# Attention with experts: two gates on SyncE's DMAs, at the query and the key group

## What is computed

```python
x = L0_attn_x                                   # [32, 512, 256], fp32
xn = layernorm(x)
# attention, 16 heads of 16, no softmax:
q, k, v = xn @ Wq + bq, xn @ Wk + bk, xn @ Wv + bv      # split into heads
scores = einsum('bhid,bhjd->bhij', q, k) * decay_mask   # 0.95 ** (i - j), causal
out = einsum('bhij,bhjd->bhid', scores, v)
attn = groupnorm(out @ Wo + bo) * gamma + beta          # a group is a head, over all positions
# 8 experts, each takes the 128 best of the 512 rows of each batch:
probs = softmax(xn @ gate_w)
top_p, top_idx = top_k(probs.T, 128)
ffn = scatter_add(top_idx, top_p * (gelu(xn[top_idx] @ w1) @ w2))
return x + attn + ffn
```

## Time and profile before

| what | us |
|---|---|
| median of three executions | 2489.22 (2487.41 to 2489.69) |
| the profiled execution | 2482.65 |
| its span, first to last instruction | 2480.8 |
| PE busy | 2323.8 (94%) |
| PEld, DVE, POOL, ACT busy | 2024.0, 1305.8, 1277.9, 990.0 |
| DMA share of the queue of SyncE's transfers (q1) | 10.8% of 16 engines |

### The profile page before, as it was taken

The page is one execution under the profiler, slowest core; times in us unless marked ns, Lnnn a source line. Parts: engine busy times, 40 slices in busy tenths (PEclk is TensorE's granted clock), DMA queues, the critical chain, the costliest instruction groups (busy, mean ns, idle before and its releaser), DMA issues.

```text
span 2480.8 us, 76765 instructions
## 1 busy us (share of the span) xinstructions
PE 2323.8 (94%) x31948; PEld 2024.0 (82%) x31948; DVE 1305.8 (53%) x2531; ACT 990.0 (40%) x1801; POOL 1277.9 (52%) x2088
## 2 busy tenths in 40 slices
PE   6999999889999995899999999999999999999997
PEld 5777777777777773789999999999999999999996
DVE  2455545466655556764455445545544554555443
ACT  4555555555545552333333333333333333333332
POOL 4334344433343342556666666666666666665453
PEclk9999999999999997899999999999999999999998
DMA  3122222222222211322332323323223323223222
GB/s 121 54 85 73 71 71 74 85 71 78 72 79 71 71 54 50 91 43 47 78 51 44 80 47 63 65 44 82 42 49 78 49 44 81 47 47 47 45 49 26
DMA packets 129262, 156.22 MB, mean 63 GB/s; under 512 B 11008, under 2 KB 118656, under 8 KB 129024
## 3 DMA queue, kind: packets, MB, share of 16 engines
q0 software_dynamic: 49152, 67.14, 16.7%
q1 hardware_dynamic: 79872, 85.54, 10.8%
HBM read 85.53 MB, written 67.11 MB: 62 GB/s over the span
## 4 chain that ended last, share of the span: by engine, by line
PE 58%; POOL 1%; DVE 1%; issue 0%; DMA 0%; ACT 0%; POOLq 0%; DVEq 0%; ACTq 0%
PE hidden L1295 28%; PE y L1310 27%; PE xt L1282 2%; POOL out L1148 0%; POOL xg L1138 0%; DMA out<-y,scatter_idx 0%; DVE best_index L204 0%; DVE g_hi L1262 0%; DVE best L200 0%; DMA xg<-xn_rows,step_idx 0%; DVE g_lo L1264 0%; DVE rows L208 0%; DVE xt_lo L1251 0%; ACT y L1197 0%; ACT g L1211 0%
## 5 line engine op out<-in xcount | busy, mean ns | idle before, releaser
L1148 POOL DMA_INDIRECT out<-y,scatter_idx x256 | 430.7, 1683 | 412.1 <-ACT y L1197 352.6
L1262 DVE CAST g_hi<-g 128x512 fp32r<-128x512 f32 x512 | 289.7, 566 | 667.6 <-ACT g L1211 665.2
L1310 PE MATMUL y<-w_hi,g_hi 128*128 128x256 f32 x2048 | 571.3, 279 | 0.3 <-ACT y L1197 0.3
L1310 PE MATMUL y<-w_lo,g_hi 128*128 128x256 f32 x2048 | 565.8, 276 | 0.0
L1310 PE MATMUL y<-w_hi,g_lo 128*128 128x256 f32 x2048 | 565.6, 276 | 0.0
L1211 ACT ACTIVATE g<-hidden 128x512 f32<-128x512 f32 x512 | 306.8, 599 | 402.9 <-PE hidden L1295 402.9
L1295 PE MATMUL hidden<-xt_hi,w_lo 128*128 128x512 f32 x1024 | 404.5, 395 | 0.0
L1295 PE MATMUL hidden<-xt_lo,w_hi 128*128 128x512 f32 x1024 | 402.7, 393 | 0.0
L1295 PE MATMUL hidden<-xt_hi,w_hi 128*128 128x512 f32 x1024 | 399.5, 390 | 1.5 <-DVE xt_lo L1251 1.5
L1264 DVE TENSOR_TENSOR g_lo<-g,g_hi 128x512 fp32r<-128x512 f32 x512 | 386.2, 754 | 17.6
L1310 PEld LDWEIGHTS y<-w_hi,g_hi 128*128 128x128 f32 x2048 | 384.6, 188 | 0.5 <-ACT y L1197 0.5
(11 more groups left out here) (150 smaller groups left out, 3615.1 us busy)
## 6 DMA issues: line engine op xcount, KB each, us to landing
x<-in_x SPq DMA_DIRECT2D x32, 512.0 KB, 5.6
w_stage<-in_w SPq DMA_DIRECT2D x16, 1024.0 KB, 6.1
xn_rows<-xn SPq DMA_DIRECT2D x32, 512.0 KB, 3.7
res<-in_x SPq DMA_DIRECT2D x32, 512.0 KB, 4.0
out<-res SPq DMA_DIRECT2D x32, 512.0 KB, 2.9
xg<-xn_rows,step_idx POOLq DMA_INDIRECT x256
out<-y,scatter_idx POOLq DMA_INDIRECT x256, 3.9
cst<-in_cst SPq DMA_DIRECT2D x1, 436.0 KB, 4.2
```

The source lines that it names most:

```text
L1148: pool.indirect_dma_start(out_rows, bass.IndirectOffsetOnAxis(sidx[:, k:k + 1], 0), y[:, k, :], None, compute_op=ALU.add).then_inc(scatter ...
L1262: dve.tensor_copy(g_hi[:, m, :], g32[m % 4][:]).then_inc(gh_ready, 1)
L1310: last = pe.matmul(yb[k % 2][:, 0:D], g_[:, m, cols], w[par][:, m, :], start=i == 0, stop=i == 3 * FT - 1)
```

## The change

The pair xn store and x load moves from the pass of its norm to the start of the next pass, and gets a wait for the first query group of that pass. The output store and the residual load behind it get a wait for the third group, the first key group. No instruction of another engine changes.

```diff
             def one(b, par):
+                f, l = b + 1, b + 1
+
+                if has(f):
+                    sp.wait_ge(qk_mm, 4 * f + 1)
+                if has(l):
+                    sp.wait_ge(xn_ready, TT * l + TT)
+                    sp.dma_start(xn_v[l], xn[:]).then_inc(xn_stored, 16)
+                    if has(l + 2):
+                        sp.dma_start(xb[1 - par][:], x_v[l + 2]).then_inc(x_in[1 - par], 16)
+                if has(f):
+                    sp.wait_ge(qk_mm, 4 * f + 3)
                 if has(b - 2):
                     sp.wait_ge(res_ready, 2 * b - 2)
...
                     sp.wait_ge(out_stored, max(16 * b - 16, 0))
                     sp.dma_start(res[:], x_v[b - 1]).then_inc(res_in, 16)
-                if has(b + 2):
-
-                    sp.wait_ge(xn_ready, TT * b + 3 * TT)
-                    sp.dma_start(xn_v[b + 2], xn[:]).then_inc(xn_stored, 16)
-                    if has(b + 4):
-                        sp.dma_start(xb[par][:], x_v[b + 4]).then_inc(x_in[par], 16)
```

## The result

The changed kernel took 2425.64 us, median of four executions (2415.68 to 2427.84), against 2488.31 (2482.38 to 2489.69): a ratio of 0.9747, 95% interval 0.9725 to 0.9768. That is 62.7 us less. The forecast was 2439 with a range of 2412 to 2470. The profiled execution is the fastest of the four, 2415.68 us (span 2413.9), so its trace shows some 67 us less than the one of before; where I compare traces, that is to be kept in mind.

What follows compares the result with a forecast made beforehand. The prediction took TensorE as the bound in attention, waiting for its own code, delayed by data traffic. From 2489.2 us it took 39 (stops) + 13 (clock) - 2 (new cost) = 50 us, giving 2439, range 2412 to 2470.

Steps and rivals of the forecast that it cites:

- Single stops: Attention passes with one TensorE stop for code, 2.45 us in the pass cited: expected to shrink to 1.55 us.
- the quiet pass: Attention pass after xn's stores and x's loads have run out: TensorE still stopped 1.87 us, with slow clock.
- The passes of the other kind: Attention passes with two TensorE stops, 1.14 and 1.52 us: expected to keep 1.1 us in all.
- second stops: Later stop in two-stop attention passes, 1.52 us: expected to fall to nothing, with 0.2 us allowed for a small third.
- first stops: Earlier stop in two-stop attention passes, 1.14 us: expected to keep 0.9 us, its code packet having started before the data.
- The clock: TensorE's lower clock in the 30 passes, costing 26 us: half, 13 us, expected back, bounds 0 and 26.
- the new cost: Residual load delaying code for the block ending near 403.8, every other pass: 2 us expected, bounds 0 and 15.
- near range: Whole kernel: 2426 to 2452 us around the forecast of 2439, given chance 0.55.
- (a): Attention stops: single ones fall only to 1.87 us and keep slow clock, second ones go; 2460 us, chance 0.22.
- (b): Attention code fetch: slow by itself, data beside it chance, so nothing moves; 2489 us, chance 0.07.
- (c): Attention: single stops stay and a late residual load adds stops at the block ending near 403.8; 2526 us, chance 0.06.
- (d): Attention passes: nearly all stops and all the clock loss go; 2412 us, chance 0.10.

Runs made afterwards that it cites:

- e5: Changed kernel plus two 512 KB DRAM-to-DRAM copies at the old place of xn store and x load, touching no tile: 2477.89 us.
- e7: Changed kernel with 162 waits on an already reached semaphore instead of one ahead of TensorE's first matmul, adding 80 instructions: 2448.16 us.
- e9: Kernel before, SyncE's old order, with only TensorE's fourth value group moved between the first two quarters of scores times values: 2460.87 us.
- e2: Kernel before with only the output store's wait for the key group added; xn store and x load stay: 2491.66 us.
- e1: Changed kernel without the output store's wait for the key group; xn store and x load still moved: 2425.57 us.

## Why the prediction was right

**The bound and the cause.** PE bound, waiting for its own code, delayed by data beside it: e5 shows that traffic alone brings the stops back, e7 that they follow the blocks. The "mostly hidden" of the Trainium skill (Runtime: NRT & Kernel Launch, Instruction fetch mechanics) stays untrue here, with 36.4 us left with no traffic beside them.

**The stops.** Expected 39 us saved, measured 42.1 (78.5 to 36.4), in the second trace of the changed kernel 38.1. Under this sum two errors partly cancel, which is luck. Single stops, expected 1.55, came out between 0.5 and 1.5, 1.10 in the mean of the table above, so 0.45 too high. About half of that is the work in the block: the prediction took 2.0 us, though its own block start near 403.9 and stop at 406.05 give over 2.1, and the table has 2.2. Its 1.1 from block start to packet is 0.9, its 2.45 from packet to resumption 2.4. I had leaned towards the quiet pass, whose 1.87 was a slow sample: no stop of the changed kernel's first trace is over 1.5. The passes of the other kind, expected at 1.1, kept 1.25 in the mean. Their second stops went as expected: L920's 14.3 us became 1.7. Their first stops stayed, at 0.9 on the average of a pass from 350 us on (0.5 to 1.1), and a third was left in some, up to 0.97.

**The clock.** This term was mis-sized: half of 26 us was expected, and 26.4 (61.4 x 0.43) came back in the profiled execution, 22 in the second (10.2 us left). The half was a hedge: the prediction had seen the clock fall behind a stop of 1.87 and put its own 1.55 below that. The runs bear out no such bound: the clock fell behind a stop of 1.68 in the second trace of the changed kernel and behind 1.25 in e9, and held behind 1.47 in the first. That all of it came back there is in part luck. The term accounts for 9 to 13 of the 13 us by which 2439 was too high. In the profiled execution, for which the forecast was 17 too high, 13.4 are the clock, 3.1 the stops and 2 the new cost, while 2.2 were lost in the column "remains" of the ledger.

**The range.** 2425.64 lies in the range of 2412 to 2470, and just at the low edge of the near range, 2426 to 2452, that had been given 0.55.

**New costs.** 2 us expected at the block that is wanted 0.3 us after its packet is in; no stop stands before L857's or L874's successors (L862, L879) in the 30 passes, so 0. Nobody came late for xn, x or res: no such wait is in PE's list, though the last data lands up to 14.9 us into a pass instead of before 14.5.

**The rivals.** (a), 2460, fell with the single stops. (b) and (c) needed the traffic to be chance; e5 rules that out, and the residual load never met the block that (c) names: in those passes the last data is in by +13.6, and the block starts at +14.1. (d), 2412, was nearer than I gave it, 14 us off like the forecast itself: its clock half came true, its stops did not. The second gate, which the prediction did not cost apart from the first, is worth nothing by itself (e2) and beside it (e1).

## What to carry to other kernels

When an engine's waits are released by nothing the profile shows and stand at even distances in its instructions, look at the instruction queue and at what else is in the DMA queues at that moment. In an unrolled program keep bulk transfers out of stretches of many short matmuls, even transfers that nobody waits for, and issue them where few long instructions run. Slow instructions mixed into such a stretch can help as well: 12 moved ones brought another 10 to 14 us here.

## What was not expected of the hardware

That where the block ends fall matters as much as a whole transfer: with 78 instructions of padding ahead of the passes the code waits in them rise to 52.8 us (36.4 and 40.4 without), and with the store at its old place to 52.7. And one transfer of 512 KB beside a tight block lengthens its stop nearly as much as two (2.15 and 2.29 us in the mean against 2.51, with 1.10 for none); the second costs more in the other blocks and in the clock.
